# AdaLN-FFN kernel: stencil tiles and layer-2 even rows laid out in one piece per partition, first loads reordered, result stores behind loads

## The reference, cut to what matters

```python
# y = cond(x), per image b, with zX, zY, zR of that image
y = zX * lap_x(x) + zY * lap_y(x) + zR * x * (1.0 - x)      # reflecting edges
# ffn(y)
lt = y[:, 1:17, :]; even = lt[:, ::2]; odd = lt[:, 1::2]
m1 = (even[:, :4, :, None] * odd[:, :4, None, :]).reshape(B, 2048, 512)
m2 = (even[:, 4:, :, None] * odd[:, 4:, None, :]).reshape(B, 512, 2048)
h = einsum('bsd,hd->bsh', y, W1) + scale * einsum('bsd,bhd->bsh', y, m1) + b1
h = gelu(h, approximate=False)
out = x + einsum('bsh,oh->bso', h, W2) + scale * einsum('bsh,boh->bso', h, m2) + b2
```

## Time and profile before

| | |
|---|---|
| median of 3 runs | 1395.82 us (1394.74 to 1396.85) |
| profiled execution, its own time | 1395.97 us |
| its span in the profile | 1394.2 us |
| PE busy | 1350.5 us (97%) |
| DVE busy | 1072.7 us (77%) |
| ACT busy | 808.9 us (58%) |
| POOL busy | 443.8 us (32%) |

### The profile page before, as it was taken

One profiled execution on the slowest core, in us unless ns is written; L12 is line 12 of the kernel. 1 busy time (PEld: TensorE's weight loads), 2 busy tenths in 40 slices (PEclk: granted clock), 3 DMA queues, 4 the chain that ended last, 5 costly groups with the idle time before them and its releaser, 6 DMA issues.

```text
span 1394.2 us, 17103 instructions
## 1 busy us (share of the span) xinstructions
PE 1350.5 (97%) x5834; PEld 1095.5 (79%) x5834; DVE 1072.7 (77%) x1681; ACT 808.9 (58%) x1406; POOL 443.8 (32%) x403
## 2 busy tenths in 40 slices
PE   7699999999999999999999999999999999999999
PEld 3488788788877788788887888877888788888887
DVE  5899878967899578995789957997688967775343
ACT  3576456754666456664566645775456655566432
POOL 4355133430354313451135501454033430133100
PEclk9899999999999999999999999999999999999999
DMA  6679587875878668776777768687587775777561
GB/s 128 152 182 230 179 229 197 184 193 178 220 194 199 188 194 194 212 192 168 220 187 208 204 187 208 172 217 184 167 230 195 187 192 189 187 200 185 146 196 53
DMA packets 192535, 262.43 MB, mean 188 GB/s; under 512 B 20416, under 2 KB 94016, under 8 KB 192448
## 3 DMA queue, kind: packets, MB, share of 16 engines
q1 hardware_dynamic: 172432, 209.82, 50.4%
q0 software_dynamic: 17664, 50.34, 20.3%
q10 hardware_dynamic: 2352, 1.20, 0.5%
HBM read 194.06 MB, written 67.24 MB: 187 GB/s over the span
## 4 chain that ended last, share of the span: by engine, by line
PE 61%; DVE 19%; DMA 11%; issue 3%; ACT 2%; SPq 0%; POOL 0%; DVEq 0%
PE po L444 12%; PE po L446 12%; PE po L445 12%; DMA W2s<-in_w_dram 10%; PE ph L427 9%; PE ph L431 9%; PE ph L429 9%; DVE W2s L412 7%; DVE W2l L419 2%; DVE y L286 1%; DVE yl L298 1%; DVE W1l L373 1%; DVE xr L520 1%; DVE y L287 1%; DVE W1l L370 1%
## 5 line engine op out<-in xcount | busy, mean ns | idle before, releaser
L444 PE MATMUL po<-W2h,gh 128*128 128x512 f32 x1024 | 400.2, 391 | 1.7 <-DVE gl L462 1.4
L446 PE MATMUL po<-W2h,gl 128*128 128x512 f32 x1024 | 399.4, 390 | 0.0
L445 PE MATMUL po<-W2l,gh 128*128 128x512 f32 x1024 | 399.4, 390 | 0.0
L427 PE MATMUL ph<-yh,W1h 128*128 128x512 f32 x896 | 353.7, 395 | 31.6 <-ACT UVs L473 20.6
L431 PE MATMUL ph<-yh,W1l 128*128 128x512 f32 x896 | 350.5, 391 | 0.0
L429 PE MATMUL ph<-yl,W1h 128*128 128x512 f32 x896 | 350.4, 391 | 0.0
L462 DVE TENSOR_TENSOR gl<-ph,gh 128x512 fp32r<-128x512 f32 x256 | 175.4, 685 | 180.1 <-ACT gh L460 179.8
L457 ACT ACTIVATE ph<-ph,b1t 128x512 f32<-128x512 f32 x256 | 167.1, 653 | 167.5 <-PE ph L431 63.2
L412 DVE SCALAR_TENSOR_TENSOR W2s<-EB,SC,W2s 128x128 f32<-128x128 f32 x512 | 214.4, 476 | 29.0 <-DMA W2s<-in_w_dram 29.0
L427 PEld LDWEIGHTS ph<-yh,W1h 128*128 128x128 f32 x896 | 168.8, 188 | 78.6 <-ACT UVs L473 20.5
L444 PEld LDWEIGHTS po<-W2h,gh 128*128 128x128 f32 x1024 | 192.7, 188 | 43.9 <-DVE gl L462 3.4
(11 more groups left out here) (85 smaller groups left out, 1280.0 us busy)
## 6 DMA issues: line engine op xcount, KB each, us to landing
R<-in_w_dram POOLq DMA_DIRECT2D x64, 512.0 KB, 9.2
W2s<-in_w_dram SPq DMA_DIRECT2D x128, 256.0 KB, 6.0
uv_scratch<-UVs SPq DMA_DIRECT2D x128, 256.0 KB, 4.3
UVs<-uv_scratch SPq DMA_DIRECT2D x128, 256.0 KB, 4.5
X<-in_xT_dram SPq DMA_DIRECT2D x56, 390.0 KB, 7.2
td_scratch<-Ts SPq DMA_DIRECT2D x64, 256.0 KB, 5.8
xr<-in_x_dram SPq DMA_DIRECT2D x16, 1024.0 KB, 7.3
xr<-in_b_dram POOLq DMA_DIRECT2D x16, 1024.0 KB, 10.6
```

Of the source, the lines that this page charges most:

```text
L427: e.matmul(bank[:, :], W1h[:, f, blk, wc], yh[:, s, c, :], start=first and c == 0, stop=False, skip_group_check=not first)
L444: e.matmul(po[t][:, :], gh[:, late, st], W2h[:, k, :], start=first, stop=False)
L445: e.matmul(po[t][:, :], gh[:, late, st], W2l[:, k, :], start=False, stop=False)
L446: mm = e.matmul(po[t][:, :], gl[:, late, st], W2h[:, k, :], start=False, stop=last)
```

## The change

- The host lays out the stencil tiles one after the other: `xT` becomes (image, tile, 128, 780), so that a partition's six rows of 130 are one run of 3120 B. A second array `xs` holds, per image, the 6 by 18 floats of each partition that `XS` needs (432 B; before, six runs of 72 B).
- The scaled even rows are written a second time, to `EQ`, laid out so that the four rows for one `EB2` are one run of 2048 B, where before `EB2` took four runs of 512 B. `k_ep` then counts both writes.
- In the head the load of `N` goes from SP's queue (fourth) to the first place of ACT's queue. The load of tile x0 goes from the first place of ACT's queue to the second of SP's, ahead of the two small `zn` loads.
- Odd tiles of W2: the fold goes from T+28 to T+35.5, the low part from T+47 to T+47.5, and the load from T-3 to T-5.5. The first `gl` of a step goes from T+37 to T+41.6.
- Result stores: the planned time was w+3t+6, and is now w+t+19 after a second half and w+t+16 after a first half.

```diff
-        k_N = d_N.dma(sp, us(0.3), [(N, bass.AP(x.tensor, 0, [[S * D, 8], [2 * D, 8], [D, 3], [1, D]]))])
+        k_N = d_N.dma(act, us(0.0), [(N, bass.AP(x.tensor, 0, [[S * D, 8], [2 * D, 8], [D, 3], [1, D]]))])
...
-        k_ep = d_ep.dma(sp, us(11.0), [(EP[:, :], N[:, 0, :])], m_ep)
+        k_ep = d_ep.dma(sp, us(11.0), [(EP[:, :], N[:, 0, :]), (bass.AP(
+            EQ.tensor, 0, [[128, 64], [8192, 4], [1, 128]]), N[:, 0, :])], m_ep)
...
-                         [(XS[:, :, :], bass.AP(xT.tensor, b * DP * SP + 1, [[4 * SP, 128], [SP, 6], [1, 18]]))],
+                         [(XS[:, :, :].rearrange("p r s -> p (r s)"), xs[b])],
...
-                load = us((0.3, 0.5, 0.4, 0.6, 1.6, 1.7, 1.8, 1.5)[n])
+                load = us((0.05, 0.5, 0.4, 0.6, 1.6, 1.7, 1.8, 1.5)[n])
...
-            kx = d_x[s].dma(act if b == 0 and n < 3 else sp, load, [(x_, bass.AP(
-                xT.tensor, b * DP * SP + 128 * n, [[4 * SP, 128], [SP, 6], [1, 130]]))], *free_x)
+            kx = d_x[s].dma(act if b == 0 and n in (1, 2) else sp, load, [(x_.rearrange("p r s -> p (r s)"), xT[b, n])], *free_x)
...
-            return (T + 28, T + 42, T + 47) if n % 2 else (T + 12.5, T + 22.5, T + 27)
+            return (T + 35.5, T + 42, T + 47.5) if n % 2 else (T + 12.5, T + 22.5, T + 27)
...
-                    EB2[:, :, :], bass.AP(EP.tensor, (8 * b + 4) * D + jk * 128, [[0, 128], [D, 4], [1, 128]]))],
+                    EB2[:, :, :].rearrange("p a q -> p (a q)"), EQ[jk, 2 * b + 1:2 * b + 2, :].broadcast_to([128, 512]))],
...
-            kd = d_w[s].dma(sp, when - (31 if n % 2 else 38), [(W2s[:, s, :], w2[k])], w2lo.at(*past2))
+            kd = d_w[s].dma(sp, when - (41 if n % 2 else 38), [(W2s[:, s, :], w2[k])], w2lo.at(*past2))
...
-            gelu(b, 0, i, 0, Y, (T + 24, T + 30.5, T + 37), c11.at(b, i))
+            gelu(b, 0, i, 0, Y, (T + 24, T + 30.5, T + 41.6), c11.at(b, i))
...
-                    stO[b, h, t] = d_o[t].dma(sp, w + 3 * t + 6, [(
+                    stO[b, h, t] = d_o[t].dma(sp, w + t + (19 if h_next == 0 else 16), [(
```

More of the change, by code:

```diff
@@ L3, with adaln_ffn_kernel @@
 from contextlib import ExitStack
-def adaln_ffn_kernel(nc: bass.Bass, xT, x, z, w1, b1, w2, b2, scale, out):
+def adaln_ffn_kernel(nc: bass.Bass, xT, xs, x, z, w1, b1, w2, b2, scale, out):
     f32 = mybir.dt.float32
@@ L14, in adaln_ffn_kernel @@
     NK, NI = 16, 8
-    SP, DP = S + 2, D + 2
     EP = nc.dram_tensor("ep_scratch", (B * 8, D), f32, kind="Internal").ap()
+    EQ = nc.dram_tensor("eq_scratch", (4, B * 2, 4 * 128), f32, kind="Internal").ap()
     UV = nc.dram_tensor("uv_scratch", (NI, 2, 128, 512), f32, kind="Internal").ap()
@@ L595, in _ @@
             dve.run(e)
-_INS = ["xT", "x", "z", "w1", "b1", "w2", "b2", "scale"]
+_INS = ["xT", "xs", "x", "z", "w1", "b1", "w2", "b2", "scale"]
 def kernel(x, condB_zX, condB_zY, condB_zR, L0_ffn_W1, L0_ffn_b1, L0_ffn_W2, L0_ffn_b2, L0_ffn_scale):
@@ L612 @@
     xT = _np.pad(x.transpose(0, 2, 1), ((0, 0), (1, 1), (1, 1)), mode="reflect")
+    xT = xT[:, 4 * _np.arange(128)[:, None] + _np.arange(6)]
+    xs = xT[:, :, :, 1:19].reshape(8, 128, 108)
+    xT = xT[:, :, :, 128 * _np.arange(8)[:, None] + _np.arange(130)].transpose(0, 3, 1, 2, 4).reshape(8, 8, 128, 780)
     data = {
-        "xT": xT, "x": x, "z": _np.stack([condB_zX, condB_zY, condB_zR], axis=1),
+        "xT": xT, "xs": xs, "x": x, "z": _np.stack([condB_zX, condB_zY, condB_zR], axis=1),
         "w1": w1, "b1": L0_ffn_b1, "w2": w2, "b2": L0_ffn_b2, "scale": _np.asarray(L0_ffn_scale).reshape(1),
```

## The result

The changed kernel takes 1370.76 us (median of 4 runs, 1369.7 to 1372.95), against 1396.28 before in the same comparison: ratio 0.9821, 95% interval 0.9804 to 0.9838. The profiled execution took 1370.56 us, with a span of 1368.8. The forecast was 1377.2: the direction was right, and the gain was 25 us, not 19. The whole of the surplus lies behind the first product.

What follows compares the result with a forecast made beforehand. Matmuls fill 1305.3 us; winnable time lies in the 40.8 us before the first product and PE's gaps after it. 1395.97 - 6.3 - 12 - 2.0 + 1.5 = 1377.2 us; own range 1371 to 1384.

Steps and rivals of the forecast that it cites:

- Part 1: Head: N first on ACT's queue, x0 second on SP's; DVE's list starts 6.3 us earlier, -6.3 (bounds 3.7 and 9.1).
- Part 2: Stencil tiles in one piece: eight tiles and N need 11.4 us in place of 17.5; nothing taken for it by itself.
- The rival by which longer runs bring no rate: Chance 0.15: tile layout gives no faster transfers; head gains 4.3 us, W2 loads and fold 10 in place of 12; 1381.2 us.
- Part 3: XS and EB2 in longer runs, EQ as a second write: k_ep delayed about 0.5 us, cost 0.
- Part 4: Stores behind loads on SP's queue: odd W2 load leaves at 233.6 in place of 235.72, 2.1 us earlier.
- Part 5: Odd W2 fold behind L373, off POOL's additions, 1.24 against 1.71 us; with the earlier load, 12 us taken (bounds 4 and 18).
- Part 6: Gap at 143.84: L373, now ahead of the fold, comes 1 to 3 us earlier; -2.0 us (bounds 0 and 3.7).
- Part 7: Later result stores: L313 waits about 2 us more; cost 1.5 us over all images (bounds 0 and 14).
- DVE as the bound: Chance 0.2: in first halves, closed gaps come back one or two steps later, only some 4 us stay; 1387.2 us.

## Why the prediction was right, and where its steps failed

**Part 1, the head.** The sum was right (6.3 forecast, 6.1 measured), but by luck: three of its steps were wrong, and the errors cancelled. The list on DVE was to start at 7.5. It started at 12.48, 1.4 us earlier than before, because the scale came at 10.94 behind x0, outside the bound of 10.13 that I had taken from the kernel before: being among the oldest transfers did not make a small load early. The stretch from L203 to L206 was to keep its length because the additions run beside it "in both orders". It went from 8.5 us to 5.8: N and x2 now let POOL start at 8.88, while DVE still waited for the scale, so POOL was 3.6 us ahead of DVE and met less of its list. The measurement with POOL held back shows the lengthening by itself (2.64 against 0.74). And x0 was to come 1 us later at no cost, as the first product waited for nothing but DVE; it came 4.5 us later, PE's stencils became what the first product follows, and the run with the zn loads first shows that x0's arrival costs.

**Part 2, the layout: the term that was mis-sized.** I took "nothing for it by itself". Alone it saves 13.4 us behind the first product, and with all other parts in place still 4.1. The step that failed is "Later tiles are used by POOL, which waits for them most of the time and hides them". POOL's wait was not hidden: it set when POOL's additions ran, and so which fold of DVE they lengthened. With the layout alone the fold's waits for W2 went from 29.0 to 0.9 us, and the odd fold of step 2 came clear of the additions. I had built the large gap mainly on the wait. The store moves alone removed that wait in step 2 and the gap stayed at 1.7 us. In image 3 of two runs (layout alone, and the changed kernel without the fold moves) there was no wait either, the additions came late, and the gap was 1.75 and 1.73. So both have to go: the load must be there, and the additions must be clear of the odd fold. How much of the 13.4 us each of the two is worth is not shown, since both come with the layout. The rival by which longer runs bring no rate is refuted: with nothing but the layout changed, a tile lands in 4.3 us in place of 7.2.
The Trainium skill (DMA: Bandwidth & Descriptors, Specifications) puts the least size for line rate at 512 B. The trace disagrees with taking runs of 520 B as free (these 7.2 and 4.3 us), and the measurement decides.

**Part 3.** The first user of an EB1 load did not wait for the second write, and `EB2` was never tried by itself, so that its cost is 0 is argued and not shown.

**Part 4, the queue.** The load does leave 2.1 us earlier after its buffer is free, as predicted. That this closes the gap is wrong, as the run with the store moves alone shows. With the layout alone the 2.1 us stay, and the fold of step 2 waits for nothing. The store moves and the earlier place of the load each remove the 2.1 us, so that neither run without one of them shows what they are worth together.

**Part 5, the fold.** It was to take 1.24 in place of 1.71 us behind L373, off POOL's additions. The 1.13 us are in the trace, but they come from the layout: the layout alone gives 1.13 at the old place, and the fold moves alone leave 1.1 to 2.0. Yet the fold moves alone save 13.2 us behind the first product. This includes the earlier place of the load and the later `gl`, which were not separated. Layout and fold moves cover for each other: 13.4 + 13.2 is more than the 19.3 of all, and leaving out either costs 4.1 or 4.4.

**The sum behind the first product.** I had 12 for parts 4 and 5 with 2 for part 6 and 1.5 against it for part 7, so 12.5 where 19.3 was measured. Image 0, from the first product to its first sum L502 of the second half (163.85 and 154.62), became 3.2 us shorter, where I had 2. The later images gave the other 16.1, where I had 12 less 1.5. The missing 6.8 us are therefore some 1.2 in image 0, 1.5 of a cost that did not come, and some 4 in the later images, about what the layout is worth beside the other parts (4.1).

**Part 6** came as predicted: the gap went, and with it a stretch at the lower clock behind it (0.51 from 145 to 148.5). **Part 7** cost nothing that PE shows: L313 waited 1.1 us over the run in place of 2.0. Against the same kernel with the stores early it is 0.5 us more, not 2 us an image.

**DVE as the bound.** This rival did not come true for the large gaps: DVE was busy 70.8 of the 75 us from 218 to 293, and PE still gained. What is left of the gaps does hang on DVE, through POOL's additions, and shifting these only shifts the gaps.

## What to carry to other kernels

A load that lands too late can be mended by making the transfers beside it cheaper: count the packets of all that share the DMA engines, not only those of the load that is waited for. An engine that waits for a late tile and seems to hide it can still cost time, by running its work beside an instruction that is on the path. When a wait is removed and the gap stays, look at how long the instruction behind the wait then takes. Take parts out one at a time and also put them in one at a time; here two edits were worth 13 us each alone and 4 each at the margin. And price an elementwise instruction by what runs beside it in its new place: an earlier start may only change which instructions of DVE and POOL meet.

## What the runs showed of the hardware

- A four-instruction fold of 128x512 on DVE took 1.13 us with POOL idle and 3.06 us beside two additions of POOL; L204 (64x512) took 0.74 and 2.64. POOL pays too: an addition L263 that takes 1.3 us took 4.19 beside DVE's low-part work in the run with POOL after the even fold.
- N, 384 KB, was the first transfer issued in both forms. With an access pattern whose outermost dimension is 8 it was first used at 8.88 us, as 64 rows at 5.99. The Trainium skill (DMA: Bandwidth & Descriptors, Rules for kernel authors) says that a transfer uses no more engines than the size of its slowest dimension allows. The two times agree with that; no row shows the engines themselves, and the runs also grew from 2048 to 6144 B, which was not separated.
- The granted clock fell to the lower of its two levels (1.2 in place of 2.4 GHz) behind the first products in both kernels (0.5 below is the lower level). Before, it was 0.51 from 46 to 53 us and 0.57 from 59.5 to 63.5, with PE idle for 5.80 us up to 49.62 and 3.22 up to 58.37. After, it was 0.51 from 41.5 to 55.5, with gaps of 4.76 and 1.94. It fell once more before, to 0.51 from 145 to 148.5, behind the gap of 2.02 us; matmuls there started 0.43 us apart in place of 0.23. Over 40 to 60 us alone, which cuts off most of the second stretch of before, the mean was 0.82 before (first line, PE's busy time alone) and 0.66 after:

```profile
40.00:60.00 20.00, 9.18 (x31) 0.82 0.62 154
```

```profile
40.00:60.00 20.00, 14.22 (x41) 10.46 (x42) 17.02 (x28) 13.40 (x25) 9.33 (x10) 0.66 0.64 140
```
